# Cross-attention of a decoder: one PSUM bank for projected keys and values, three for turned probabilities, and a ring of heads moved one head on

## The reference

```
q = (rope(x Wq + bq)) as 16 heads of 16          112 queries
k, v = rope(c Wk + bk), c Wv + bv                375 context rows, 16 heads of 16
s = (q k^T) / 8, masked;  p = softmax(s)         16 heads, 112 x 375 each
out = (p v) merged, times Wo, + bo
```

## Time and profile before

| | |
|---|---|
| median of three runs | 2056.34 us (2054.67 to 2062.97) |
| the profiled execution, whole | 2056.47 us |
| its span, first to last instruction | 2054.6 us |
| granted TensorE clock, mean over the span | 0.949 |
| first and last scores of the cross-attention loop | 530.3 and 817.0 us |
| busy share over the span: PE, DVE, ACT, POOL | 86%, 69%, 51%, 49% |

### The profile page before, as it was taken

One profiled execution on the slowest core, in us unless ns is written; L12 is line 12 of the kernel. 1 busy time (PEld: TensorE's weight loads), 2 busy tenths in 40 slices (PEclk: granted clock), 3 DMA queues, 4 the chain that ended last, 5 costly groups with the idle time before them and its releaser, 6 DMA issues. The chain is left out here.

```text
span 2054.6 us, 33436 instructions
## 1 busy us (share of the span) xinstructions
PE 1773.9 (86%) x11006; PEld 1107.5 (54%) x11006; DVE 1418.9 (69%) x2635; ACT 1045.2 (51%) x1948; POOL 1002.3 (49%) x756
## 2 busy tenths in 40 slices
PE   7967887889989999787888888888689989999799
PEld 4334444445667777443444444444554656665699
DVE  6779999993678888495555555554565348787893
ACT  4776667661788888336555554554323131114342
POOL 1269989881653321036566666665100009764342
PEclk9979999999999999899999989999899999999899
DMA  2034334433687774411556544633940044344640
GB/s 70 5 117 134 126 126 138 122 99 108 144 184 185 187 184 103 126 40 31 178 151 201 177 141 147 197 98 72 294 136 0 1 138 144 113 138 147 223 139 17
DMA packets 147377, 261.12 MB, mean 127 GB/s; under 512 B 39877, under 2 KB 104038, under 8 KB 144534
## 3 DMA queue, kind: packets, MB, share of 16 engines
q1 hardware_dynamic: 129846, 216.22, 35.7%
q0 software_dynamic: 13824, 37.77, 6.0%
q10 hardware_dynamic: 3536, 4.99, 0.9%
HBM read 205.82 MB, written 49.44 MB: 124 GB/s over the span
## 5 line engine op out<-in xcount | busy, mean ns | idle before, releaser
L3128 POOL DMA_INDIRECT moe_y<-ahead,moe_where x144 | 159.9, 1110 | 141.2 <-DVE ahead L3261 112.0
L3191 PE MATMUL moe_up_ps<-moe_w_tile,ahead 128*64 128x352 f32 x1152 | 214.3, 521 | 2.8 <-ACT moe_w_tile L3335 1.4
L2335 POOL TENSOR_TENSOR soft_power<-soft_logit,soft_high 128x1024 f32<-128x1024 f32 x28 | 66.2, 2363 | 289.3 <-DVE soft_high L2409 289.0
L3335 ACT ACTIVATE moe_w_tile<-moe_w 128x1216 f32 x144 | 175.4, 1219 | 24.1 <-issue 21.9
L3122 POOL DMA_INDIRECT ahead<-moe_tok,moe_where x144 | 144.2, 1001 | 56.9 <-issue 42.7
L1786 ACT ACTIVATE xattn_prob<-xattn_sm,xattn_least 112x375 f32<-112x375 f32 x256 | 150.8, 604 | 29.1 <-DVE xattn_least L1703 28.6
L1023 POOL TENSOR_TENSOR mamba_x_state<-mamba_x_state,mamba_cx_all 128x896 f32<-128x896 f32 x64 | 133.4, 2085 | 26.8 <-DVE mamba_x_state L1081 26.8
L3191 PEld LDWEIGHTS moe_up_ps<-moe_w_tile,ahead 128*64 128x64 f32 x1152 | 85.7, 153 | 103.1 <-issue 93.5
L1017 POOL TENSOR_TENSOR xn<-mamba_u,mamba_b_all 128x896 f32<-128x896 f32 x64 | 133.3, 2086 | 14.7 <-DMA mamba_b_all<-mamba_b 14.7
L1703 DVE CUSTOM_DVE_ANT_0 xattn_sm<-xattn_s_ps,wide 112x375 f32<-112x375 f32 x256 | 130.2, 539 | 13.0 <-PE xattn_s_ps L1592 9.7
L3255 DVE TENSOR_TENSOR moe_hid<-ahead,moe_up_ps 128x176 f32<-128x176 f32 x144 | 45.7, 333 | 133.9 <-ACT ahead L3341 82.5
(11 more groups left out here) (458 smaller groups left out, 4273.8 us busy)
## 6 DMA issues: line engine op xcount, KB each, us to landing
moe_w<-moe_w SPq DMA_DIRECT2D x64, 480.0 KB
soft_w<-soft_w SPq DMA_DIRECT2D x16, 1024.0 KB, 7.4
mamba_b_all<-mamba_b SPq DMA_DIRECT2D x32, 448.0 KB
mamba_cx_all<-mamba_c SPq DMA_DIRECT2D x32, 448.0 KB, 3.7
mamba_cy_all<-mamba_c SPq DMA_DIRECT2D x32, 448.0 KB, 4.5
moe_w_tile<-moe_y SPq DMA_DIRECT2D x14, 1024.0 KB, 8.1
soft_logits<-soft_logit SPq DMA_DIRECT2D x28, 512.0 KB, 2.6
soft_logit<-soft_logits SPq DMA_DIRECT2D x14, 1024.0 KB, 5.1
```

What stands on the lines that cost most here:

```text
L3128: pool.indirect_dma_start(y_dram, bass.IndirectOffsetOnAxis(ap=where[:, 1, t:t + 1], axis=0), y_sb[:, 2 * s + i], None).then_inc(y_stored[ ...
L3191: mm = pe.matmul(up_ps[n * HALF:(n + 1) * HALF, i, 0:2 * I], xT[:, s % 2, at:at + HALF], w_tile[:, s, i, n, h * 2 * I:(h + 1) * 2 * I], st ...
L3335: place_weights = weight_placer(act, 0, lambda to, src: act.activation(to, src, ACT.Copy))
```

## The change

PSUM: `kv_ps` shrinks to one bank, `pt_ps` grows to three. Both halves of the keys go through the one bank in turn, so half 1 waits until DVE has read half 0 (`k_half_read`). Values c = 0 and 1 lie side by side in it and are copied by one instruction (`copy_two_values`), c = 2 follows and is copied by another in iteration 0 of the next batch. Every step of a head but the copy and the product moves one head ahead: PE scores of h+7 and turn of h+3, DVE bias of h+5, ACT exponentiate of h+4. The work for later batches is placed anew, the reciprocal is cut into two halves of 112 columns, and the context's DMA is issued in ACT's iteration 5. The core of the diff:

```diff
-        RING, PT_RING, S_RING = 4, 8, 3
+        RING, PT_RING, S_RING, T_RING = 4, 8, 3, 3
-            kv_ps = k.ps(c2, "xattn_kv_ps", [P, 2, 512])
+            kv_ps = k.ps(c2, "xattn_kv_ps", [P, 512])
-            pt_ps = k.ps(c2, "xattn_pt_ps", [P, 2, 512])
+            pt_ps = k.ps(c2, "xattn_pt_ps", [P, T_RING, 512])
-            KEYS_AT, ROTATE_AT, CAST_AT = (0, 1, 2, 4), (2, 3, 5, 6), (8, 12, 14)
-            VALUES_AT, COPY_VALUES_AT = (8, 9, 10, 11, 12, 13), (11, 13, 15)
+            KEYS_AT, ROTATE_AT, CAST_AT = (1, 2, 5, 6), (3, 4, 7, 8), (10, 13, 15)
+            VALUES_AT, COPY_TWO_AT, COPY_LAST_AT = (9, 10, 11, 12, 14, 15), 13, 0
+            CONTEXT_AT, INVERT_AT = 5, (11, 13)
...
             def value_ps(c):
-                return kv_ps[0:KC, c % 2, c // 2 * D:(c // 2 + 1) * D]
+                return kv_ps[0:KC, c % 2 * D:(c % 2 + 1) * D]
...
+                    if m == 1 and h == 0:
+
+                        pe.wait_ge(k_half_read, b)
...
-                        pe.wait_ge(v_read, CK * b + 1)
+                        pe.wait_ge(v_read, CK * b + 2)
...
-                    if h >= 2:
-                        pe.wait_ge(*copies(b, h - 2))
+                    if h >= T_RING:
+                        pe.wait_ge(*copies(b, h - T_RING))
...
-                        ahead(b, s, h + 6, scores)
-                        ahead(b, s, h + 2, turn_probs)
+                        ahead(b, s, h + 7, scores)
+                        ahead(b, s, h + 3, turn_probs)
...
-                        ahead(b, s, h + 4, bias_scores)
+                        ahead(b, s, h + 5, bias_scores)
...
-                        if h == 12 and precedes(b):
-                            invert(b - 1, 1 - s)
+                        if h in INVERT_AT and precedes(b):
+                            invert(b - 1, 1 - s, INVERT_AT.index(h))
...
-                        ahead(b, s, h + 3, exponentiate)
+                        ahead(b, s, h + 4, exponentiate)
...
+                        if h == CONTEXT_AT and follows(b, 3):
+
+                            act.wait_ge(v_ready, CK * (b + 1))
+                            load_context(act, b + 3)
...
-                        if follows(b) and h in COPY_VALUES_AT:
-                            copy_values(b + 1, 1 - s, COPY_VALUES_AT.index(h))
+                        if follows(b) and h == COPY_TWO_AT:
+                            copy_two_values(b + 1, 1 - s)
+                        if precedes(b) and h == COPY_LAST_AT:
+                            copy_last_values(b, s)
```

More of the change, by code:

```diff
@@ L1674, in _ @@
                 pe.wait_ge(q_kept, 3)
-                for h in range(6):
+                for h in range(7):
                     scores(0, 0, h)
-                for h in range(2):
+                for h in range(3):
                     turn_probs(0, 0, h)
@@ L1690, in rotate_keys @@
                     table = (k_cos, k_sin, k_sin, k_cos)[n]
-                    product = dve.scalar_tensor_tensor(turn[:, n], kv_ps[:, m, 0:S2], bk[:, m:m + 1], table, ALU.add, ALU.mult)
+                    product = dve.scalar_tensor_tensor(turn[:, n], kv_ps[:, 0:S2], bk[:, m:m + 1], table, ALU.add, ALU.mult)
+                    if n == 1:
+                        product.then_inc(k_half_read, 1)
                     if n == 3:
@@ L1755, in _ @@
                     dve.scalar_tensor_tensor(bo_centred[:, m:m + 1], bo[:, m:m + 1], bo_mean[:, 0:1], bias_ps[:, 2 + m:3 + m], ALU.subtract, ALU.add)
-                for h in range(4):
+                for h in range(5):
                     bias_scores(0, 0, h)
@@ L1759, in _, with copy_two_values, copy_last_values @@
                 batches(dve, batch)
-                invert(B - 1, 1)
+                for m in range(DH):
+                    invert(B - 1, 1, m)
             @block.scalar
             def _(act):
-                def copy_values(b, s, c):
-                    if c == 0:
-                        wait(act, pv_done, QUADS * (b - 1))
-                    act.wait_ge(v_ready, CK * b + c + 1)
-                    if c == CK - 1 and follows(b, 3):
-                        load_context(act, b + 3)
-                    act.activation(v[:, s, c, :, 0::2], value_ps(c).rearrange("p (h d) -> p h d", d=HD), ACT.Copy).then_inc(v_read, 1)
+                def copy_two_values(b, s):
+                    wait(act, pv_done, QUADS * (b - 1))
+                    act.wait_ge(v_ready, CK * b + 2)
+                    act.activation(v[:, s, 0:2, :, 0::2], kv_ps[0:KC, 0:2 * D].rearrange("p (c h d) -> p c h d", c=2, d=HD), ACT.Copy).then_inc(v_read, 2)
+                def copy_last_values(b, s):
+                    act.wait_ge(v_ready, CK * (b + 1))
+                    act.activation(v[:, s, 2, :, 0::2], value_ps(2).rearrange("p (h d) -> p h d", d=HD), ACT.Copy).then_inc(v_read, 1)
                 def cast_keys(b, n):
@@ L1850, in _ @@
                 cast_queries(OTHERS, 1)
-                copy_values(0, 0, 2)
+                copy_last_values(0, 0)
                 keep_queries(4)
@@ L1854, in _ @@
                 cast_queries(OTHERS, 2)
-                for h in range(3):
+                for h in range(4):
                     exponentiate(0, 0, h)
```

28 lines of the change are left out of this document (15 added, 13 removed).

## The result

The changed kernel takes 2100.8 us (median of four runs, 2092.8 to 2101.6) where the kernel before takes 2058.2 on the same chip (2054.7 to 2063.0): 42.6 us more. The ratio with its 95% interval, taken over all runs and not from the two medians (whose quotient is 1.0207), is 1.0196 [1.0178, 1.0215], or 40 us. The side was forecast, the size was not: 2100.8 lies above the range of 2050 to 2088. The profiled execution of after is 2101.4 us with a span of 2099.5, 44.9 more than that of before.

The account below looks back on a forecast made before the run. It took a loop across batches (head 0's scores, third key cast, store, loads, next scores) as the bound. First leg +1.4 and second -0.2 give +1.2 us, times 13 loops 15.6: 2072 us, +0.8%, range 2050 to 2088.

Parts of the forecast that it names:

- The side: Whole kernel: slower 0.62, same 0.29, faster 0.09, with a measurement telling apart about 0.5%, or 10 us.
- The loop that I named: Attention batches: head 0's scores, third key cast, store, loads, next batch's scores set the pace, 17.71 us each.
- The waits of DVE that vanished: DVE's copies behind PE's transposes, 21.3 us: cost time only as far as they lengthen one of the two legs.
- First leg: From head 0's scores to the end of the third key cast: 7.4 instead of 6.0 us, +1.4 a loop.
- Second leg: From the third cast through store and loads to the next scores: -0.2 us a loop, bounds -1.4 and +1.2.
- Prologue 0: Prologue does one head more and the last batch one less: 0 added.
- The early loops: Three early batches: reciprocal still starts when the sums land, same new order behind it, so the same +1.2 us each.
- PE's own pace: PE in steady batches without the wait for key loads: 17.7 less 1.1, or 16.6 us a batch.
- faster: Rival: three banks let the ring run ahead, first leg falls to 5.8, PE's 16.6 bounds: -13, 2043 us; chance 0.10.
- No change: Rival: DVE waits vanish, first leg +1.2, second -1.0, so 3 us over 13 loops: 2059 us; chance 0.20.
- It doesn't do what it says: Rival: copies still wait, first leg gets two iterations more, +1.9 a loop, +25: 2081 us; chance 0.07.
- The context in the tail: Rival: context's DMA passes whole in the key loads' tail, second leg +0.9, +30 in all: 2086 us; chance 0.13.

Follow-up runs that it names:

- the loop cut: Key loads read the parts stored by the batch before, so they wait for no cast of their own batch: after 1.0008, before 0.9933, against before.
- the sums out of the way: After with the two halves of the reciprocal in iterations 14 and 15 instead of 11 and 13: 1.0141 against before.

## Why the prediction was wrong in size, point by point

The loop that I named was the bound, and the side was right. The size failed at the terms of the sum: it took every duration at the upper clock, it put the prologue, the first and the last batch at nothing, and it gave the early loops the same +1.2 us as the steady ones.

**The loop as the bound: right.** The wait for the keys went from 1.1 to 2.2 us a batch (2.3 forecast), and with the loop cut after runs at 17.50 us a batch. The waits of DVE that vanished brought nothing, as was said. The last key load landed 0.04 us before head 0's scores in nearly every batch of after.

**First leg: right in kind, its floor nearly so (7.4 forecast, 7.57 measured with the sums out of the way).** But the steps in between were placed otherwise. I had exp 17 at 2.85 us, the values copy waiting for PE until 4.7. Exp 17 started at 4.02 in the loop shown, because bias 17 stands behind half a reciprocal that waited 0.57 us for the sums, and the values copy followed the second cast without a gap. Even without that wait bias 17 would have been late: bias 16 began at 1.12 and not at 0.45, for DVE began to write the mask (0.68 us) only 0.22 us after the scores of head 0 had started. The sums were in my upper bound (+0.5) and belonged, at 0.2, in the value. The term is +1.76 where I had +1.4.

**Second leg: right in size (-0.13 measured, -0.2 forecast), by luck.** The third store lands in 3.1 us (3.4 forecast, 4.2 on average before):

```profile
DMA to landing us min/median/max: 3.1/3.1/3.1
```

So the store gives 1.1 us where I had 0.7. The last load takes 6.4 to 9.4 us where I had 6.7 to 7.2, on average 7.8 in the steady loops (6.8 before), which takes 1.0 back. I had put 0.5 there, for the context, but with the context moved it still takes 7.7. The two errors cancel. The 200 to 290 GB/s that I took from the earlier trace rows are a misreading as well: its two lines have 288 and 164.

**The clock: missing from the sum.** It was the largest mistake, and the step that failed. All my durations were at the granted clock 1.00 of the earlier trace rows, and I never asked what PE's longer wait does to it. Three of ten steady first legs are 2.2 us longer on average than the rest (6.7 us in all), and the last batch takes 17.2 us, 14.7 where PE was kept busy. The first loop (half clock in 552 to 559) takes 21.1 us, 19.6 with three further matmuls, and 2.7 us of the prologue are the clock's. That makes some 13 of the 44.9 us, besides what is in the early loops.

**"Prologue 0": wrong, +4.0.** I had costed the half of the keys that waits for DVE only in the loop, where it hides. In the prologue nothing stands between the two halves: PE waits 1.3 us, and the clock comes up 7 us later, which costs 2.7 more.

**The early loops: wrong, +2.9 each instead of +1.2.** I had let the reciprocal start when it did before. The last of the sums lands 6.0 to 6.4 us after the scores instead of 3.8 to 4.9, though SP begins to issue them at about the same place, and 1.5 us more hang behind the reciprocal. Taking the reciprocal out of the way removed 3.0 us of each loop. Why the sums land later stays open: moving the context, which is under way beside them, didn't bring them back (6.8 to 7.2).

**PE's own pace: wrong, 16.6 for 17.29.** A wait taken off an engine in the trace didn't give the pace without it. That the engines ahead of it use the pause too is my reading, not shown. It cost the forecast nothing, but it made the rival "faster" look possible. With 17.50 for the new ring it never was.

**The sum.** 13 loops x 1.2 = 15.6 became 31.7 (8.7 early, 23.0 steady), 2.4 us each. My own bound was +2.6, but the 2084 that I wrote as its end is only +2.1 a loop, so the range was narrower than its terms. The steady 23.0 are 17.6 for the undisturbed first leg (14 forecast), 6.7 for the clock and -1.3 for the second leg (-2 forecast). Outside the loops I counted lie another 12.4 ahead of the last scores, put at nothing: 0.9, 4.0, 1.1, 2.9 and 3.5.

**The rivals.** No change needed a second leg that is 1.0 us shorter, faster a first leg that falls. "It doesn't do what it says" falls with DVE's wait at 0.3 us. The context in the tail gave a time near the truth (2086) for a reason that the moved context refutes. No rival held the true combination: the forecast's own loop, with the clock and the prologue on top.

**Open.** The alternation of the last load's landing (6.5 and 8 to 9 us) was not explained, nor why waits of 3.1 and 2.6 us ended without a fall of the clock where others of 3.4 and 2.7 had one. The 0.9 us ahead of the stage lie in stages that the change doesn't touch; that distance is 503.6 to 507.3 us over all traces here. The first batch's 1.1 and 1.4 of the first loop's 2.9 were not taken apart. The last 1.0 us of the last batch (14.7 with the clock kept, or the loop cut, against 13.7) is the new order's; it was not taken apart.

## What to carry to other kernels

Before giving a ring more lead, look for a round trip across batches: count the iterations from the consumer's first step to the producer's last, because the lead lengthens that leg while the DMAs' part of it stays. Price a shared bank in the prologue too, where nothing stands between its two uses, and look at the clock behind the wait. And when a change lengthens a wait of PE, sum the loop again at the lower clock.

## What the runs showed of the hardware that I had not expected

- **A longer wait of PE costs twice.** Behind some of PE's waits for the keys (3.35, 4.03 and 2.65 us, but not behind 3.13 and 2.62) the granted clock fell to 0.50 (1.2 GHz). The batch behind it then lost 1.5 to 2.7 us on its critical leg (9.24 to 10.50 instead of 7.77). In the prologue a wait of 1.3 us was followed by 2.7 us lost to a clock that came up at 521.4 us instead of 514.1. The Trainium skill ("TensorE: Matmul & The Clock Gate", HAM oscillation) tells of loops that fall back to the lower level at each wait for a DMA; here it was some of the passes, about 48 us at the lower level in all.
- **Three matmuls more for PE in each batch made the kernel faster, six made it slower** (1.014 and 1.025 against 1.019 to 1.022; six beside after, three in another group of runs).
- **A store that landed sooner was paid back by the loads behind it.** The same third store landed in 3.1 us instead of 4.2 on average, and the last of the same four loads in 7.8 instead of 6.8, so the second leg moved by 0.1 us.
- **A context load of 375 KB beside the key loads cost them nothing that can be seen** (12.56 us with it, 12.69 without). It gave way itself: 8.0 us to its landing (median) instead of 3.6.
